# Equal token halves, another split of the weight preparation and a reordered tail in the first MoE of a fused block

## The reference, cut to what matters

```python
# x: 4 x 1024 tokens of 256 values, float32
x = x + 0.5 * ffn(layernorm(x))         # "first MoE", tag a
x = x + retention_block(layernorm(x))   # two layers, tag l
x = x + 0.5 * ffn(layernorm(x))         # "second MoE", tag b, the same weights

def ffn(h):                             # E = 16 experts, TOPK = 2, KS = 3
    probs = softmax(h @ router_w + router_bias)
    top_w, top_i = top_k(probs, 2)
    norm_w = top_w / (sum(top_w) + 1e-6)
    combine = sum(one_hot(top_i, 16) * norm_w[..., None], axis=1)
    routed = combine[:, 15:16] * h      # expert 15 is the identity
    for e in range(15):
        y = silu(h @ gate_w[e]) * (h @ up_w[e]) @ down_w[e]     # 256 -> 128 -> 256
        routed = routed + combine[:, e:e+1] * y
    gate = causal_conv1d(h, conv_w)     # 3 taps, 256 -> 128
    shared = silu(gate) * (h @ shared_up_w) @ shared_down_w
    return shared + routed
```

## Time and profile before

| | us |
|---|---|
| runs | 1434.94, 1437.10, 1439.26 |
| profiled execution | 1430.13 |
| its span | 1428.3 |
| first MoE, head: start to the first matmul of a pair | 0 to 96.2 |
| pair loop of the first MoE | 96.2 to 244.9 |
| tail of the first MoE, to the first matmul of the retention | 244.9 to 312.9 |
| second MoE, pair loop: first and last product | 1233.9 to 1370.5 |

### The profile page before, as it was taken

The page is one execution under the profiler, slowest core; times in us unless marked ns, Lnnn a source line. Parts: engine busy times, 40 slices in busy tenths (PEclk is TensorE's granted clock), DMA queues, the critical chain, the costliest instruction groups (busy, mean ns, idle before and its releaser), DMA issues.

```text
span 1428.3 us, 30726 instructions
## 1 busy us (share of the span) xinstructions
PE 1313.4 (92%) x11828; PEld 1084.5 (76%) x11828; DVE 1006.0 (70%) x2371; ACT 605.1 (42%) x1023; POOL 599.5 (42%) x480
## 2 busy tenths in 40 slices
PE   3789989756999999999999899999999999999997
PEld 2469888435788788788788688788788776799964
DVE  5855473668876876876876877887887878655745
ACT  5426555411333433433424333333433656666631
POOL 4767330751332331341441542452463437272635
PEclk9899999879999999999999999999999999999999
DMA  9988695940000000000101000000000138586844
GB/s 332 357 282 258 213 322 200 310 127 2 1 1 2 1 2 1 2 1 2 35 13 60 2 1 2 16 16 2 16 16 2 31 98 321 184 271 214 270 136 151
DMA packets 115211, 152.55 MB, mean 107 GB/s; under 512 B 12288, under 2 KB 97664, under 8 KB 115072
## 3 DMA queue, kind: packets, MB, share of 16 engines
q1 hardware_dynamic: 100672, 114.93, 24.5%
q0 software_dynamic: 12288, 33.57, 7.1%
q10 hardware_dynamic: 2112, 2.10, 0.5%
HBM read 77.56 MB, written 73.01 MB: 105 GB/s over the span
## 4 chain that ended last, share of the span: by engine, by line
PE 61%; DVE 14%; ACT 1%; issue 1%; POOL 0%; DVEq 0%; ACTq 0%
PE l_w_ps L84 9%; PE l_w_ps L86 8%; PE l_w_ps L85 8%; DVE l_probs L2053 5%; PE l_banks L2314 4%; PE l_rm_ps L2346 3%; PE l_banks L84 2%; PE l_banks L85 2%; PE l_banks L86 2%; PE l_rm_ps L2339 2%; PE b_gu_ps L84 2%; PE b_gu_ps L85 2%; PE b_gu_ps L86 1%; DVE l_f_lo L2084 1%; PE b_t_ps L1302 1%; DVE l_full L2015 1%
## 5 line engine op out<-in xcount | busy, mean ns | idle before, releaser
L2053 DVE TENSOR_TENSOR l_probs<-l_banks,l_past 128x512 f32<-128x512 f32 x256 | 160.1, 683 | 33.6 <-PE l_banks L2314 33.5
L1813 ACT ACTIVATE l_act_f<-l_w_ps,l_ffn_b 128x512 f32<-128x512 f32 x120 | 82.6, 689 | 169.1 <-PE l_w_ps L86 164.3
L1904 POOL TENSOR_TENSOR l_g_lo<-l_q,l_g_hi 128x1024 fp32r<-128x1024 f32 x16 | 38.2, 2386 | 264.9 <-ACT l_g_hi L1804 264.9
L84 PE MATMUL l_w_ps<-l_w_hi,l_f_hi 128*128 128x256 f32 x496 | 143.6, 290 | 2.6 <-DVE l_f_lo L2084 2.4
L86 PE MATMUL l_w_ps<-l_w_hi,l_f_lo 128*128 128x256 f32 x496 | 139.6, 281 | 0.0
L85 PE MATMUL l_w_ps<-l_w_lo,l_f_hi 128*128 128x256 f32 x496 | 139.5, 281 | 0.0
L819 POOL DMA_INDIRECT a_picked<-rows,a_pos_i x64 | 64.4, 1006 | 94.8 <-issue 72.7
L1891 POOL TENSOR_TENSOR l_q_wide<-l_q,l_pair_mask 128x1024 f32<-128x1024 f32 x32 | 60.1, 1898 | 103.1 <-DVE l_q L2031 103.1
L84 PE MATMUL l_w_ps<-l_b_hi,l_w_hi 128*128 128x512 f32 x240 | 102.5, 427 | 0.3 <-ACT l_f_hi L1814 0.3
L84 PEld LDWEIGHTS l_w_ps<-l_w_hi,l_f_hi 128*128 128x128 f32 x496 | 93.3, 188 | 8.8 <-issue 8.7
L2084 DVE TENSOR_TENSOR l_f_lo<-l_act_f,l_f_hi 128x512 fp32r<-128x512 f32 x128 | 85.9, 702 | 18.4 <-ACT l_f_hi L1814 18.4
(11 more groups left out here) (424 smaller groups left out, 4007.3 us busy)
## 6 DMA issues: line engine op xcount, KB each, us to landing
rows<-a_zeros SPq DMA_DIRECT2D x16, 1024.0 KB, 13.6
a_xb<-rows SPq DMA_DIRECT2D x46, 256.0 KB, 3.5
rows<-a_yb SPq DMA_DIRECT2D x46, 256.0 KB, 3.2
b_xb<-rows SPq DMA_DIRECT2D x46, 256.0 KB, 3.2
rows<-b_yb SPq DMA_DIRECT2D x46, 256.0 KB
a_w_in<-in_moe_w SPq DMA_DIRECT2D x15, 384.0 KB, 12.8
low_dram<-a_w_lo SPq DMA_DIRECT2D x15, 384.0 KB, 4.4
b_w_lo<-low_dram SPq DMA_DIRECT2D x15, 384.0 KB, 9.3
```

What stands on the lines that cost most here:

```text
L84: tensor.matmul(out, w_hi, x_hi, start=start, stop=False)
L1813: nc.scalar.activation(act_f[:, f, :], hidden_ps(b, f), ACT.Gelu, bias=ffn1_b[:, b.layer, f:f + 1]).then_inc(act_done, 1)
L2053: dve.tensor_tensor(probs[c % 2][:, r * w:(r + 1) * w].rearrange("p (h n) -> p h n", n=P), banks[:, r, :].rearrange("p (h n) -> p h n", n= ...
```

## The change

The parts of the first MoE become 16 and 16 columns: 46 blocks and 16 more each. The zeros that cover blocks only the second MoE's larger parts would use are not needed any more. GpSimd splits no weights: ScalarE makes all 15 high parts, VectorE all 15 low parts. VectorE normalises tiles 1 and 3 of the first MoE. SyncE loads the weights, then writes zeros for part 0 and for all but the last three copies of part 1, then loads the first four pairs, and then writes those three. The positions of part 1 are worked out inside the pair loop, as in the second MoE. In the tail each tile's shared result is added before the combines of the tile, and work for the retention is moved. The wait for the last stores of x_sb moves into the retention part.

```diff
-A_BATCHES = (range(0, 3), range(3, 6), range(6, 8))
-PLAN_A = plan_of((12, 20), 4, 8, A_BATCHES, A_BATCHES, (range(0, 1), range(1, 3), range(3, 5), range(5, 8)))
+SINGLE = tuple(range(t, t + 1) for t in range(NT))
+PLAN_A = plan_of((16, 16), 4, 8, (range(0, 4), range(4, 8)), SINGLE, SINGLE[0:4] + (range(4, 6), range(6, 8)))
...
-            chunks += [(HALVES, b, r, min(CLEAR, ROWS[b] - r)) for b in range(HALVES) for r in range(sizes[b], ROWS[b], CLEAR)]
...
-            if begins:
-                load_piece(0)
             sp.dma_start(w_sh[:, :], weights[:, 0:SHARED_COLS]).then_inc(shared_loaded, 16)
             if begins:
                 sp.wait_ge(zeros_set, 1)
-                for n in range(1, PIECES):
+                for n in range(PIECES):
                     load_piece(n)
                 for chunk in chunks:
-                    if chunk[0] < HALVES:
+                    if chunk[0] == 0:
                         clear(chunk)
+                second = [chunk for chunk in chunks if chunk[0] == 1]
+                for chunk in second[:-3]:
+                    clear(chunk)
...
             for q in range(XB):
                 load_block(q)
+            if begins:
+                for chunk in second[-3:]:
+                    clear(chunk)
...
-                for chunk in chunks:
-                    if chunk[0] == HALVES:
-                        clear(chunk)
...
             sp.wait_ge(stored_first, 16)
-            sp.wait_ge(stored, 16 * (NT - 2 + SUB))
+            if ends:
+                sp.wait_ge(stored, 16 * (NT - 2 + SUB))
...
# GpSimd
-            else:
-                for n in range(POOL_LO):
-                    if n < POOL_HI:
-                        high_weights(n)
-                    low_weights(n)
...
# VectorE, before the pair loop
+                for n in range(0, 4):
+                    low_weights(n)
                 run(place_blocks(0))
+                shared_product(1)
+                for n in range(4, 7):
+                    low_weights(n)
+                add_shared(0)
+                shared_product(2)
+                for n in range(7, 13):
+                    low_weights(n)
+                shared_product(3)
+                soften(1)
+                add_shared(1)
+                share(1)
+                run(choose(1, 0))
+                add_shared(2)
+                run(choose(1, 1))
+                mark(1)
+                for n in range(13, PIECES):
+                    low_weights(n)
+                add_shared(3)
+                later = rest()
...
-                if ends:
-                    next(later, None)
+                next(later, None)
...
# TensorE
             if begins:
-                for n in (POOL_LO - 1, PIECES - 1):
-                    low_ready(pe, n)
+                pe.wait_ge(dve_lo_done, PIECES)
...
-                if ends and n == 0:
+                if n == 0:
                     count(1)
...
# retention, SyncE and VectorE
                 sp.dma_start(x_old[:, :, :], view[0]).then_inc(x_old_in, 16)
+                sp.wait_ge(x_stored, 16 * (NT - 2 + SUB))
...
+                dve.wait_ge(x_stored, 16 * (NT - 2 + SUB))
                 normalise_0(whole(1))
```

More of the change, by code:

```diff
@@ L548, in sync @@
             if begins:
-                for of in range(HALVES + 1):
+                for of in range(HALVES):
                     sp.wait_ge(cleared[of], 16 * sum(chunk[0] == of for chunk in chunks))
@@ L875, in invert, with normalise @@
                                          ALU.mult).then_inc(shift_done, 1)
+            def normalise(t):
+                dve.wait_ge(shift_done, group_of(t) + 1)
+                for s in range(SUB):
+                    c = t * SUB + s
+                    last = dve.tensor_scalar(normal(c), x_sb[:, c, :], rstd[:, c:c + 1], mv[:, c, 0:1], ALU.mult, ALU.add)
+                last.then_inc(xn_odd_done, 1)
             def wide(v, n):
@@ L996, in add_shared @@
                 dve.wait_ge(s_acc_done, t + 1)
-                if FRONT <= t < NT - begins:
+                if ends and t >= FRONT:
                     dve.wait_ge(x_done, (t + 1) * SUB)
@@ L1028, in combine @@
             def combine(c):
-                dve.wait_ge(shared_added, NT if begins and c >= COLS - SUB else min(c // SUB + 1, FRONT))
+                dve.wait_ge(shared_added, c // SUB + 1 if begins else min(c // SUB + 1, FRONT))
                 dve.wait_ge(picked_in[c % PICKED], 32 * (c // PICKED + 1))
@@ new lines, in vector @@
+            dve.wait_ge(signals[3], 2)
+            dve.wait_ge(acc_done, NPAIRS)
+            apply_ahead(dve, ahead, x_sb, lambda s: home.xn[:, s, :]).then_inc(first_xn, 1)
+            low_home(range(0, 2))
+            finish(range(20, 22))
+            low_home(range(2, 4))
+            finish(range(22, 24))
+            shared_product(7)
+            low_home(range(4, 6))
+            dve.wait_ge(first_turned, 1)
+            dve.wait_ge(consts_in, 16 * len(consts))
+            for k in range(KD):
+                last = dve.tensor_scalar(home.full[:, k, :], first_ps[:, k, :], home.norm1[:, 0, 0, k:k + 1],
+                                         home.norm1[:, 0, 1, k:k + 1], ALU.mult, ALU.add)
@@ L1234, in turn @@
                     pe.wait_ge(xT_done, t - 1)
+                if begins and not late:
+                    if t == 5:
+                        pe.wait_ge(lg_read, 1)
+                    if t == 6:
+                        pe.wait_ge(sh_done, 2)
+                    if t == 7:
+                        pe.wait_ge(shared_added, 1)
                 if ends and not late:
@@ L1265, in turn_logits @@
                 pe.wait_ge(lgT_done, i + 1)
[L1266 to L1267 removed]
+                if begins and i == 1:
+                    pe.wait_ge(planned, 1)
                 n = QUAD * len(BATCHES[i])
@@ L1322, in shared_down @@
                     pe.wait_ge(shared_added, t)
+                if begins and t == 1:
+                    pe.wait_ge(xT_done, NT)
                 for s in range(SUB):
```

229 lines of the change are left out of this document (99 added, 130 removed).

## The result

The changed kernel takes 1443.93 us (median of 6, 1443.29 to 1448.77), the kernel before beside it 1434.75 (median of 6, 1431.2 to 1439.26). The ratio is 1.0071, 95% interval 1.0056 to 1.0087: slower, by 9 to 10 us where 4.7 were forecast. The direction holds, and so does the mechanism of the head; loop and tail gave back less than forecast.

The account below looks back on a forecast made before the run. TensorE's matmuls fill most of the span; DMA bytes, then GpSimd's scatters hold the first pair, VectorE the changed tail. 10.0 + 1.5 - 3.2 - 3.6 = +4.7 us on 1437.1 gives 1441.8, own range 1437 to 1447, over all 1432 to 1450.

Parts of the forecast that it names:

- steps 1 and 2: Head: part 0's extra zeros start the scatters 3.6 us later; with 32 scatters the first load goes out 10.0 us later.
- step 4: Loop start: TensorE's idle time brings the lower clock, slowing the first pairs: +1.5 us, bounds 0 and 2.5.
- step 5: Pair loop: SyncE's stall on part 1's scatters goes, about 1 us returned for planning inside the loop: -3.2 us.
- step 6: Tail: fewer combines on VectorE, new waits for gates of tiles 5 and 6, store wait leaves the barrier: -3.6 us.
- upper bound for VectorE's subtractions: Head: eight low-part subtractions beside scatters each stretch one by 0.47 us, 3.8 us, counted only in the upper bound.
- Step 3: Head: extra weight parts on ScalarE and VectorE, two tiles VectorE normalises and the freed GpSimd, all costed at nothing.
- the store's 1.2 us: End of the tail: the wait for the last store to land leaves the barrier, 1.2 us less.
- is no earlier: Tail: the gate of tile 6, at 276.42 + 0.6, hangs on loads and was taken to come no earlier.
- A: Rival, tail: GpSimd's picks bound it, so it falls by 10.6 us and the store's 1.2; -3.5 us, 1433.6; chance 0.16.
- B: Rival, head: zeros don't hold part 0, landing before 53.5, load 2.5 us earlier; -9.3 us, 1427.8; chance 0.10.
- C: Rival, loop start: loads 4 to 7 starve behind fresh zeros, scatters stretch; +10.7 us, 1447.8; chance 0.22.

Follow-up runs that it names:

- E1: Changed kernel with part 0's eight copies of zeros behind the first four weight pieces instead of all fifteen: 1436.52 us, 1.0007 of the kernel before.
- E2: Changed kernel without the last 8 of part 0's 32 scatters, their rows staying zero: 1435.95 us, 0.9999 of the kernel before.
- E6: Changed kernel with 165 unused transposes on TensorE ahead of the pair loop: 1.0043 of the kernel before.
- E10: Changed kernel with part 0's zeros earlier, low-part copies in the head, 88 unused transposes and tail weights ahead of constants: 0.9950 of the kernel before.
- E5: Changed kernel with the 15 copies of low weight parts to DRAM moved into the head, run three times: 0.9975, 0.9983 and 0.9984 of the kernel before.
- E3: Changed kernel with 110 unused transposes on TensorE ahead of the pair loop: 1443.41 us, 1.0054 of the kernel before.
- E4: Changed kernel with the tail's seven retention weight pieces issued ahead of the 24 small constants: 1442.53 us, 1.0044 of the kernel before.
- E8: Kernel before, with only the wait for the last stores of x moved from the first MoE's end into the retention: 0.9997 of the kernel before.
- E11: Changed kernel unaltered, run again on a slower chip: 1615.5 us, 0.9982 of the kernel before beside it.

## Why the prediction was right, and where it fell short

The cause of the later start was right and well sized. That 1443.93 lies within 2.1 us of the forecast time, 1441.8, is in part luck: the kernel before came out at 1434.75 in six runs, not at 1437.1 as in three. As a difference the forecast is about half of what was measured, and the measured difference (9.2 or 10.2) lies at the upper end of the forecast's own range, 0 to +10. All errors of the steps go the same way.

The sum to the start of the retention, in us against the trace of before. Loop and tail are means over the traces on the first chip that share the code (five in the loop, four in the tail):

| step | forecast | measured |
|---|---|---|
| first load (steps 1 and 2) | +10.0 | +10.9 |
| clock, by the first gate (step 4) | +1.5 | +2.0 |
| pairs 0 to 30 (step 5) | -3.2 | -2.0 (92.6 for 94.6) |
| pairs 30 to 45 | 0 | +1.7 (50.1 for 48.3) |
| tail to the retention (step 6) | -3.6 | -1.8 (70.2 for 72.05) |
| sum | +4.7 | +10.8 |

The runs say +9.2 by the medians and +10.2 by the ratio. The column of before is one trace, which lies 4.6 us below its median, and the same code took 48.8 to 50.8 us in pairs 30 to 45 and 69.1 to 71.5 in the tail. So the last two rows are good to 1 or 2 us, not better.

Steps 1 and 2 are right in cause and size. The zeros started the scatters (E1) and each scatter costs its pitch (E2). The positions were there at 45.0, so the whole difference from 54 to 58 is bytes. The 4 us that the prediction had in its upper bound for VectorE's subtractions did not come: with eleven of them beside it the row of 32 scatters took 42.6 us, the second MoE's 42.1. That they can stretch it showed in E1, where fifteen lie beside it: 43.9.

Step 3, the work that lies beside, is right: ScalarE's and VectorE's weight parts are done at about 75 and 86, and TensorE's head at 85. The freed GpSimd gained nothing, because it waited for zeros.

Step 4 has the right cause and too small a size: 2.1 to 2.5 us from turn to gate and not 1.5, shown by the same stretch at the full clock (E6, E10). The assumption that the first pairs wait for other engines anyway was wrong there: from turn to gate TensorE waits 1.2 us for VectorE, 1.0 before, and the rest is its own chain of matmuls, which all follow each other more slowly.

Step 5: pairs 15 to 30 gave 4.0 us back (44.9 for 48.9), and gates 15 to 18 account for it, where the kernel before stalled: 12.5 us before, 8.6 now. The first five pairs took 16.5 instead of 14.8; of these 1.8 us, 1.0 is the planning inside the loop, since the second MoE, in the same order, takes 15.8 in the kernel before, and the rest the clock (0.6 in E6). What the step left out are pairs 30 to 45. I compared only up to pair 30. Part 0's picks begin at 188 instead of 164, and end at 230 instead of 195; the copies of the low parts to DRAM run from 194 to 242 (182 to 229 before). So 36 us of picks lie beside copies where 12 did. Windows of the changed kernel, then of the kernel before:

```profile
200.00:210.00 10.00, 7.77 (x57) 7.49 (x56) 5.81 (x13) 4.02 (x9) 7.56 (x9) 0.88 1.05 378
220.00:230.00 10.00, 7.96 (x68) 7.70 (x67) 6.50 (x14) 4.87 (x11) 6.00 (x7) 1.00 1.02 368
230.00:240.00 10.00, 8.93 (x76) 8.58 (x75) 7.20 (x16) 5.66 (x13) 0.00 (x0) 1.00 0.98 344
```
```profile
210.00:220.00 10.00, 10.00 (x87) 9.91 (x87) 5.84 (x13) 6.46 (x14) 0.00 (x0) 1.00 0.88 294
220.00:230.00 10.00, 8.68 (x74) 8.41 (x72) 4.61 (x9) 5.46 (x13) 0.00 (x0) 1.00 0.74 258
230.00:240.00 10.00, 9.65 (x80) 9.12 (x79) 4.71 (x10) 6.12 (x14) 0.00 (x0) 1.00 0.31 108
```

In the changed kernel the DMA engines stay full until 240, and TensorE has two gaps of over 2 us that nothing in the profile ends, where the kernel before has one of 2.4:

```profile
207.09 0.38 PE L84 MATMUL a_gu_ps<-a_w_hi,a_bx_hi 128*128 x1 [2.23 <-issue]
222.31 0.38 PE L84 MATMUL a_gu_ps<-a_w_hi,a_bx_hi 128*128 x1 [2.04 <-issue]
```

That the overlap of picks and copies makes them is argued, not shown. The run that would have told it (E5) fell thrice on chips where this stretch is longer anyway, and there it gained nothing without the copies. The same code in E3 and E4 has no gap of over 1.6 us there and took only 0.9 and 0.5 us more than before.

Step 6: the store's 1.2 us are right (1.1 in the changed kernel, 1.3 in E8). The combines gave 0.7 instead of 2.4, since "is no earlier" was the wrong bound for the gate of tile 6: it came later. SyncE issued l_wr 14.2 us behind the first product and not 12.1 (changed kernel, then before):

```profile
280.88 0.44 SPq L533 DMA_DIRECT2D l_wr<-in_reto_w  x1
```
```profile
265.38 0.44 SPq L529 DMA_DIRECT2D l_wr<-in_reto_w  x1
```

Of this, 1.3 us come from the fourth tile that part 0 now has to store ahead of the weights, and E4 shows that these loads hold the tail. The prediction took this gate's time from the earlier trace rows as fixed and did not follow SyncE's queue, in which the fourth store now stands ahead. The step's sum has a slip too: by its own times the second idle time is 277.02 - 272.4 = 4.6 us, not 5.3. It was 6.86, and the first 8.31 where 7.8 were forecast.

The rivals. A, the tail belongs to GpSimd: no, VectorE waits for gates, and GpSimd waits 7.8 us for VectorE's combines. B, its condition: zeros by 53.5; they landed at 57.9. With the zeros moved (E1) its first half comes true, and even then the kernel is only as fast as before. C, the loop starves behind the late zeros: no pair among 2 to 5 waits for a load. Its change (+10.7) is nearer to the measured 9 to 10 than my +4.7, but for other reasons; its time (1447.8) is farther off than mine.

What stays open: from the retention's start to the second MoE's loop the changed kernel took 925.3 us and E1 to E4 922.9 to 925.1, the one trace of before 920.5. With this the traces would put the change at 13 us and more, where the runs say 9 to 10; the low trace of before may be the reason. Part of it is where the clock falls among the short matmuls of the retention's start; windows of before (first) and of the changed kernel (second):

```profile
330.00:335.00 5.00, 2.96 (x48) 2.02 (x48) 4.92 (x17) 0.30 (x1) 0.00 (x0) 0.66 0.01 3
335.00:340.00 5.00, 3.40 (x82) 2.61 (x82) 4.09 (x9) 0.00 (x0) 0.00 (x0) 1.00 0.00 0
```
```profile
345.00:350.00 5.00, 2.49 (x26) 1.60 (x30) 4.29 (x10) 0.00 (x0) 0.00 (x0) 0.50 0.02 3
350.00:355.00 5.00, 4.67 (x78) 3.44 (x72) 2.73 (x5) 0.00 (x0) 0.00 (x0) 0.57 0.00 2
```

From the retention's first matmul to its first product with l_wr it took 41.1 us there and 43.7 here, and 41.7 to 44.0 in the other kernels; this alone would spread a kernel's runs by up to 3 us.

## What to carry to other kernels

Equal halves move work from the second part to the first, and whatever stands ahead of the first load pays the full pitch (1.3 us a scatter here), while the wait of 7.4 us that they shorten had been half hidden: 4.0 us came back. Ask first which queue holds the start, and empty that: moving eleven weight loads behind the zeros gave back 7 of the 9 us. And when a stretch of SyncE's list gets one item longer, follow each later item to the engine that waits for it, to the end of the loop and not just as far as the stall.

## What the runs showed of the hardware

On three other chips every kernel took 12 to 13% longer, the one before too, all of it in the two MoEs: from the retention's start to the second MoE's first scatter E11 took 871.6 us, the changed kernel on the first chip 873.5. The head of the first MoE ran as on the first chip (first scatter at 57.7, first load at 101.7 in E11). But in the loop the engines stood still while GpSimd issued scatters. Windows of the changed kernel there (E11), then its waits from 125 to 170 us:

```profile
120.00:130.00 10.00, 9.88 (x84) 9.59 (x83) 6.24 (x18) 4.69 (x10) 3.93 (x5) 1.00 0.54 174
150.00:160.00 10.00, 0.00 (x0) 0.00 (x0) 0.00 (x0) 0.00 (x0) 7.56 (x9) 0.50 0.39 139
170.00:180.00 10.00, 9.17 (x57) 9.18 (x58) 4.19 (x8) 5.39 (x12) 0.00 (x0) 0.69 0.36 109
```
```profile
PE a_acc_ps L84 <- issue: 21.1, 1, 21.1
DVE a_bh_lo L1029 <- issue: 20.8, 2, 17.4
ACT a_yb L671 <- remote: 15.0, 2, 12.7
```

Three engines at once wait for nothing that the profile names, at a DMA share of 0.39. The last scatter ends at 165.2, and TensorE runs on at 167.35. From pair 5 to pair 7 it took 43.0 us instead of 6.6. Pairs 15 to 30, which have the first picks in them, took 61.8 us instead of 45.3, and the second MoE's pairs 198.4 instead of 138.7. The Trainium skill, in "Runtime: NRT & Kernel Launch", section "Instruction fetch mechanics", says that each sequencer streams its own code by DMA and that the cost is mostly hidden. If late code is what the engines waited for, it was not hidden here; no run isolates it, so the cause is open.

The standstills may be why the change costs nothing there, but this is argued and not shown. In E8, which has the order of before, the 40 scatters of part 1 stood in the way of the loop's first pairs (28 us from gate 0 to gate 1; first gate at 120.5, in E11 at 110.95), and the tail with 40 picks took 77.6 us from first product to retention, in E11, with 32, 64.3. Against that, the loop from gate 0 to gate 45 was shorter in E8, 185.9 us for 200.0. So what a balance of halves is worth depends on the chip that runs it: 1.0071 on the first, 0.9982 on another.
